# Attention scores added in PSUM to negated maxima that ScalarE copies there

## The reference, cut to what matters

```python
q = (x @ Wq).reshape(b, s, N_HEADS, HEAD_DIM)
k = (x @ Wk).reshape(b, s, N_HEADS, HEAD_DIM)
v = (x @ Wv).reshape(b, s, N_HEADS, HEAD_DIM)
dot = jnp.einsum('bihd,bkhd->bhik', q, k)
w = jax.nn.softmax(dot / jnp.sqrt(jnp.float32(HEAD_DIM)), axis=-1)
a = jnp.einsum('bhij,bjhd->bihd', w, v)
return a.reshape(b, s, N_HEADS * HEAD_DIM) @ Wo + bo
```

## Time and profile before

| | us |
|---|---|
| median of 3 runs | 1869.91 (1866.15 to 1872.6) |
| the profiled execution | 1864.58 |
| its span | 1863.3 |
| first add to the start of the last in the attention | 438.9 to 1703.1 |

### The profile page before, as it was taken

How to read it: one execution, slowest core, us unless ns; L and a number is a source line. 1 busy time by engine, 2 the same in 40 slices (tenths; PEclk the granted TensorE clock), 3 DMA queues, 4 the chain that set the end, 5 groups by cost and what they waited for, 6 DMA issues and landing times.

```text
span 1863.3 us, 34439 instructions
## 1 busy us (share of the span) xinstructions
PE 1660.9 (89%) x13785; PEld 979.6 (53%) x13785; DVE 1191.0 (64%) x1984; ACT 805.3 (43%) x1235; POOL 1306.9 (70%) x670
## 2 busy tenths in 40 slices
PE   4888852858999999999999999999999999995695
PEld 3666641745555555555555555555555555553475
DVE  2666666566666766666766666766666766653476
ACT  2555520444444444444444444444444444443223
POOL 2333322415988988988889888889888999995422
PEclk9877755879999999999999999999999999997698
DMA  8000000210000000000000000000000000000312
GB/s 244 4 3 3 4 1 16 64 33 1 1 1 1 1 1 1 1 1 1 1 1 1 1 1 1 1 1 1 1 1 2 1 1 1 1 1 28 98 41 73
DMA packets 33238, 29.76 MB, mean 16 GB/s; under 512 B 3676, under 2 KB 28752, under 8 KB 33080
## 3 DMA queue, kind: packets, MB, share of 16 engines
q1 hardware_dynamic: 24664, 19.38, 3.5%
q0 software_dynamic: 2496, 5.13, 0.8%
q10 hardware_dynamic: 5920, 3.04, 0.8%
HBM read 18.33 MB, written 9.21 MB: 15 GB/s over the span
## 4 chain that ended last, share of the span: by engine, by line
PE 79%; DVE 9%; POOL 6%; issue 3%; ACT 2%; DMA 1%; ACTq 1%; POOLq 0%; DVEq 0%; SPq 0%
PE psum L1895 24%; PE psum L1880 18%; PE psum L1853 9%; PE psum L1877 6%; POOL a_acc L2181 3%; PE psum L1525 2%; PE psum L1903 2%; PE psum L1826 2%; PE psum L1487 1%; POOL y_rows L1090 1%; DVE a_mx L2060 1%; PE psum L465 1%; PE psum L1535 1%; PE psum L375 1%; PE psum L470 1%
## 5 line engine op out<-in xcount | busy, mean ns | idle before, releaser
L2181 POOL TENSOR_TENSOR a_acc<-a_acc,a_Pb 128x1024 f32<-128x1024 f32 x448 | 1066.5, 2380 | 115.9 <-ACT a_Pb L1997 60.4
L2060 DVE TENSOR_REDUCE a_mx<-psum 128x2 f32<-128x1024 f32 x512 | 626.0, 1225 | 372.2 <-PE psum L1853 369.4
L1997 ACT ACTIVATE a_Pb<-psum 128x1024 f32<-128x1024 f32 x512 | 497.7, 1024 | 568.9 <-PE psum L1880 568.9
L1895 PE MATMUL psum<-a_Pb,a_Vb 128*64 128x512 f32 x2048 | 494.1, 603 | 0.0
L1895 PEld LDWEIGHTS psum<-a_Pb,a_Vb 128*64 128x64 f32 x2048 | 127.0, 136 | 231.4 <-issue 180.1
L1853 PE MATMUL psum<-a_Kh,a_Qh 64*128 64x512 f32 x1024 | 234.1, 451 | 5.4 <-DVE a_mx L2060 5.1
L1853 PEld LDWEIGHTS psum<-a_Kh,a_Qh 64*128 64x128 f32 x1024 | 97.6, 184 | 229.6 <-issue 219.9
L1877 PE MATMUL psum<-a_Mr,a_ones_r 64*128 64x512 f32 x1024 | 203.3, 392 | 0.0
L1880 PE MATMUL psum<-a_Ql,a_Kh 64*128 64x512 f32 x1024 | 202.4, 390 | 0.0
L1880 PE MATMUL psum<-a_Qh,a_Kh 64*128 64x512 f32 x1024 | 202.2, 390 | 0.0
L1880 PE MATMUL psum<-a_Qh,a_Kl 64*128 64x512 f32 x1024 | 201.8, 388 | 0.0
(11 more groups left out here) (393 smaller groups left out, 1944.2 us busy)
## 6 DMA issues: line engine op xcount, KB each, us to landing
x_rows<-att_raw ACTq DMA_DIRECT2D x2, 1483.5 KB, 24.4
g_w<-in_L_ffn_w_eDF_dram SPq DMA_DIRECT2D x2, 1408.0 KB, 9.0
r_W<-in_L_ffn_W_dram SPq DMA_DIRECT2D x1, 2048.0 KB, 14.0
r_tile_x<-x_rows SPq DMA_DIRECT2D x23, 64.5 KB
g_tile_x<-x_rows SPq DMA_DIRECT2D x23, 64.5 KB
y_all<-y_rows SPq DMA_DIRECT2D x4, 256.0 KB, 4.3
g_w<-in_L_ffn_w_eFD_dram SPq DMA_DIRECT2D x2, 512.0 KB, 10.2
g_xg<-y_rows SPq DMA_DIRECT2D x4, 256.0 KB, 3.7
```

What stands on the lines that cost most here:

```text
L1895: last = pe.matmul(ps[HEAD[h], B_O, :], b.Vb[:, p // 2 % 2, kc, at], b.Pb[:, step % BUFS, h * QT:(h + 1) * QT], start=(kc == 0), stop=(kc ...
L1997: act.activation(b.Pb[:, step % BUFS, :], ps[:, slot:slot + 2, :].rearrange("p a b -> p (a b)"), ACT.Exp, scale=SCALE).then_inc(S["probs"], 1)
L2060: v.tensor_reduce(b.mx[:, :, qc, quarter:quarter + 1], ps[:, bank:bank + 2, :], AX.X, ALU.max).then_inc(S[f"free{bank}"], 1)
L2181: g.tensor_tensor(b.acc[:, u, :], before, b.Pb[:, step % BUFS, :], ALU.add).then_inc(S["added"], 1)
```

## The change

The product of ones with `Mr` goes, and with it `Mr`, `ones`, `mask` and VectorE's multiplication. A score tile instead begins as a copy of the negated maxima that already lies in its banks, and the three products a head are added to it (no product of a step has `start=True`).

- At d = 7 TensorE writes the next unit's negated maxima into banks 0 and 1 with eight products of 128 columns (`seed`: a column of `nm`, broadcast, times the unit matrix). It waits for the exponential that reads these banks last. This seeds step 0 of the unit. For the first unit sixteen products fill both slots.
- ScalarE copies the two banks to SBUF (`guard`, into `Mb`, two buffers).
- For every other step ScalarE copies `Mb` into the banks of the step, behind the exponential that emptied them (`seed` of ScalarE): after the two exponentials of a round it seeds both slots for the next.
- VectorE's four reciprocals come a place earlier (d = 1, 2, 2, 3 instead of 2, 2, 3, 3); between the last of them and `normalise` there is now a reduction.
- VectorE could seed steps too, but the set `SEED_DVE` that names them is empty.

```diff
-            if R:
-                pe.wait_ge(S["probs"], 2 * R - 1 + i)
-            for h in range(2):
-                pe.matmul(ps[:, slot + h, :], b.ones[HEAD[h], :], b.Mr[HEAD[h], :], start=True, stop=False)
+            who, n = plan.seeded[2 * R + i]
+            if who != "pe":
+                pe.wait_ge(S[f"seeded_{who}"], n)
...
-                    last = pe.matmul(ps[:, slot + h, :], K[HEAD[h], p % 2, at], Q[HEAD[h], U % 3, :], start=False, stop=(n == 2))
+                    last = pe.matmul(ps[:, slot + h, :], K[HEAD[h], p % 2, at], Q[HEAD[h], U % 3, :], start=False, stop=(n == 2), skip_group_check=True)
...
-    def mask(U):
-        if U == 0:
-            pe.wait_ge(S["ident_r"], 1)
+    def seed(U):
+
         pe.wait_ge(S["negated"], U + 1)
-        bank = begin(("mask", U))
-        end(pe.matmul(ps[:, bank, 0:P], b.nm[:, :], b.ident[:, :], start=True, stop=True), bank)
+        begin(("seed", U))
+        if U:
+            pe.wait_ge(S["probs"], NT * U - 1)
+        else:
+            pe.wait_ge(S["free2"], plan.before[2])
+        for first in ((0, 2) if U == 0 else (0,)):
+            for h in range(2):
+                for qc in range(4):
+                    last = pe.matmul(ps[:, first + h, qc * P:(qc + 1) * P], bcast(b.nm[:, h, qc:qc + 1], [P, P]), b.ident[:, :],
+                                     start=(qc == 0), stop=(qc == 3), skip_group_check=True)
+        end(last, 0)
...
+    def guard(U):
+        bank = begin(("seed", U))
+        if U > 1:
+            for who in ("act",):
+                act.wait_ge(S[f"seeded_{who}"], max(n for step, (w, n) in plan.seeded.items() if w == who and step < NT * (U - 1)))
+        act.activation(b.Mb[:, U % 2, :], ps[:, 0:2, :].rearrange("p a b -> p (a b)"), ACT.Copy).then_inc(S[f"free{bank}"], 1)
+
+    def seed(step):
+        U, slot = step // NT, 2 * (step % 2)
+        if plan.seeded[step][0] == "act":
+            bank, n = plan.at["seed", U]
+            act.wait_ge(S[f"free{bank}"], n)
+            act.wait_ge(S["probs"], step - 1)
+            act.activation(ps[:, slot:slot + 2, :].rearrange("p a b -> p (a b)"), b.Mb[:, U % 2, :], ACT.Copy).then_inc(S["seeded_act"], 1)
...
+        if seed_job(R):
+            guard(U + 1)
+        for step in (2 * R + 2, 2 * R + 3):
+            if step < STEPS:
+                seed(step)
...
         if U and d in (2, 3):
-            invert(U - 1, 2 * d - 4)
+            invert(U - 1, 2 * d - 3)
         if U and d == 4:
             normalised_low(U - 1)
         if early:
             maximum(*early[1:])
-        if U and d in (2, 3):
-            invert(U - 1, 2 * d - 3)
+        if U and d in (1, 2):
+            invert(U - 1, 2 * d - 2)
+        if 2 * R + 3 < STEPS:
+            seed(2 * R + 3)
```

More of the change, by code:

```diff
@@ L1696, in misc_job, with seed_job @@
         return "v", p // 2 + 1, U % RN
-    if d == 7 and U < UNITS - 1:
-        return "mask", U + 1
-    return None
+    return None
+def seed_job(R):
+    U, d = R // RN, R % RN
+    return ("seed", U + 1) if d == 7 and U < UNITS - 1 else None
 def max_jobs(R):
@@ L1705, in max_jobs, with seeder @@
     return [("max", U, 2 * i + j) for j in range(2)] if U < UNITS else [None, None]
+SEED_DVE = ()
+def seeder(step):
+    if step % NT == 0 or step == 1:
+        return "pe"
+    return "dve" if step % 2 and (step // 2 - 1) % RN in SEED_DVE else "act"
 class Plan:
@@ L1723, in __init__ @@
                 self.job(("v", 0, m // 2), (B_O, B_P)[m // 2 % 2])
-        self.job(("mask", 0), B_P)
+        self.job(("seed", 0), 0)
         for key in max_jobs(-1):
@@ L1734, in __init__ @@
                 self.job(misc_job(R), B_P)
+            if seed_job(R):
+                self.job(seed_job(R), 0)
+        self.seeded, n = {}, {"pe": 0, "act": 0, "dve": 0}
+        for step in range(STEPS):
+            who = seeder(step)
+            n[who] += 1
+            self.seeded[step] = who, n[who]
         for key in (("sum", UNITS - 1), ("out", UNITS - 1)):
@@ L1766, in allocate_attention @@
     b.Qh, b.Ql = (sb(a, [P, 3, QT], F32R) for a in ("Qh", "Ql"))
-    b.Mr = sb("Mr", [P, QT], F32R)
-    b.ones = sb("ones_r", [P, P], F32R)
-    b.mask = sb("mask", [P, 4, P])
+    b.Mb = sb("Mb", [P, 2, 2 * QT])
     b.Vb = sb("Vb", [P, 2, NT, 2 * P])
@@ L1867, in scores @@
         if d == 0:
-            freed(("mask", U))
+            freed(("seed", U))
             freed(("q", U))
@@ L1915, in misc @@
         kind, *at = key
-        {"k": keys, "out": output, "sum": sums, "v": values, "q": queries, "mask": mask}[kind](*at)
+        {"k": keys, "out": output, "sum": sums, "v": values, "q": queries}[kind](*at)
     pe.wait_ge(S["tile_yt"], SLOTS_T)
@@ L1935, in attention_pe @@
             values(0, m // 2)
-    mask(0)
+    seed(0)
     for _, U, m in max_jobs(-1):
@@ L1950, in attention_pe @@
             misc(misc_job(R))
+        if seed_job(R):
+            seed(*seed_job(R)[1:])
         if R:
@@ L2017, in attention_act @@
         values(0, j)
+    guard(0)
     for R in range(ROUNDS):
@@ L2066, in negate, with seed @@
         if U:
-            bank, n = plan.at["mask", U - 1]
+            bank, n = plan.at["seed", U - 1]
             v.wait_ge(S[f"full{bank}"], n)
[L2069 to L2075, removed]
+        v.tensor_reduce(b.nm[:, :, :], b.mx[:, :, :, :], AX.X, ALU.max, negate=True).then_inc(S["negated"], 1)
+    def seed(step):
+        U, slot = step // NT, 2 * (step % 2)
+        if plan.seeded[step][0] == "dve":
+            bank, n = plan.at["seed", U]
+            v.wait_ge(S[f"free{bank}"], n)
+            v.wait_ge(S["probs"], step - 1)
+            v.tensor_copy(ps[:, slot:slot + 2, :].rearrange("p a b -> p (a b)"), b.Mb[:, U % 2, :]).then_inc(S["seeded_dve"], 1)
     def invert(U, part):
@@ L2140, in attention_dve @@
             maximum(*early[1:])
-        if U and d in (2, 3):
-            invert(U - 1, 2 * d - 3)
+        if U and d in (1, 2):
+            invert(U - 1, 2 * d - 2)
+        if 2 * R + 3 < STEPS:
+            seed(2 * R + 3)
         key = misc_job(R)
-        if key and key[0] in ("q", "k", "mask", "out"):
-            {"q": queries, "k": keys, "mask": mask, "out": output}[key[0]](*key[1:])
+        if key and key[0] in ("q", "k", "out"):
+            {"q": queries, "k": keys, "out": output}[key[0]](*key[1:])
         if U and d == 3:
```

12 lines of the change are left out of this document (3 added, 9 removed).

## The result

| | before | after |
|---|---|---|
| median of six runs, us | 1870.5 (1858.0 to 1874.0) | 1879.0 (1871.6 to 1880.6) |
| profiled execution, us | 1864.6 | 1877.9 |
| first add to end of the last, us | 1266.6 | 1275.0 |
| one unit, sums to sums (mean of 14), us | 40.00 | 40.29 |

The ratio of after to before is 1.0053, with a 95% interval of 1.0028 to 1.0078. The forecast was 1823 us. The table has two quantities that I use from here on. The stages ahead of the attention have nearly the same code in all kernels, yet the first add began anywhere from 438.9 to 451.2 us. So kernels are compared by the time from the first add to the end of the last, and by the unit in the middle of the run, as a mean of 14. Single units lie within 0.04 us of it before the change and within 0.03 after.

The account below looks back on a forecast made before the run. TensorE was taken as the bound, with GpSimd's adds close behind as a 37.9 us floor. 1864.6 - 55.2 (GpSimd's idle) + 0.2 x 32 + 2 at the start = 1818, plus 5.3 to the median: 1823 us, range 1807 to 1850.

Parts of the forecast that it names:

- TensorE's round: Bare rounds (d = 2 and 3): TensorE's products take 3.9 us, level with ScalarE's 3.9 from scores to scores.
- in the others TensorE has 0.9 us more to do, which covers it: Rounds with another job: TensorE's 0.9 us of extra products hide ScalarE's chain of exponentials and seed.
- Up to five copies of 512 columns: ScalarE's other copies in a unit: 2.5 us at a pitch of 0.50, within ScalarE's total of 32.5 us.
- the floor: GpSimd's fifteen adds a unit, each waiting for the one before: no unit under 37.9 us, whatever other engines do.
- the seed's price on ScalarE: One ScalarE copy of 1024 columns from SBUF into PSUM: taken as 0.96 us, about 1.0 to 1.05 alone.
- the seeding products: TensorE's eight products of 128 columns a unit: 0.9 us taken, 0.5 to 1.1 possible; sixteen at the start, 3.2 us.
- the wait at d = 7 of about 0.35: At d = 7 TensorE's seeding products wait about 0.35 us for the round's first exponential, and no more is lost.
- VectorE's line from the sums to the subtraction: Reciprocals, reductions, normalising and ScalarE's copy: the subtraction that frees bank 7 comes 13.4 us after the sums.
- rival 4: TensorE's clock falls to 1.2 GHz in places; a tenth of its time there gives 41.8 us a unit, 1926; chance 0.04.
- the query product waits for the subtraction, 0.5 to 1.0 a unit: Sign of a right forecast: TensorE's query product waits 0.5 to 1.0 us a unit for VectorE to free bank 7.
- The slower side: Chance 0.10 of a slower run: drawn-out ScalarE writes to PSUM, a falling TensorE clock, or a share of eaten savings.
- Rival 1: Hand-overs between ScalarE and TensorE make bare rounds 4.2 to 4.4 us and a unit 39.0; 1848 us, chance 0.17.

Follow-up runs that it names:

- the half reductions: The changed kernel with each maximum reduced over the first 256 of 512 columns of either bank: one run, 1830.0 us, a unit of 38.63 us.

## Why the prediction was wrong

**The step that failed is the one on TensorE's round**: "TensorE's shortest round is 0.43 + 1.38 + 0.23 + 1.87 = 3.9" and "in the others TensorE has 0.9 us more to do, which covers it". The round was added up from TensorE's products and compared with ScalarE's chain. The loop through VectorE was never closed for an ordinary round. The rows had most of it. The late product starts at 1002.61 and its reduction ends at 1004.31, 1.70 us later, against the 0.43 + 1.38 = 1.81 that TensorE works before the early product. That leaves 0.11 for a hand-over, which no row there shows and the prediction put at nothing. Measured after the change by the starts of the products: 1.77 us to the end of the reduction and 0.14 of hand-over make 1.91, against 1.74 of work, a wait of 0.17, and the weighing behind it comes another 0.11 late. The 0.9 us of the other job cover none of it, for they stand behind the early product.

The prediction had followed this line only from the sums to the query product. That piece came out as forecast, 13.57 us against 13.5, and the waits at d = 2 and 3 lie inside it. At d = 7 the wait for the exponential covers the loop, and this round took 5.28 with the half reductions too. What the loop adds to a unit is about 0.3 us in each of the four rounds at d = 5, 6, 0 and 1: some 1.2 us, and 1.36 with all that shorter reductions gave (39.30 to 37.94).

**A second step is missing altogether.** The seeds were priced by what they make late on TensorE (the scores), not by what they stand ahead of on ScalarE. "Up to five copies of 512 columns" entered the sum as work; that keys and queries pass from them to VectorE, with a reduction queued behind, was not asked. Measured: 0.99 us a unit, the whole of the second pattern.

With both the unit is 40.29 - 0.99 - 1.36 = 37.94, the floor. GpSimd's floor left 2.06 us a unit to win (40.00 to 37.94). TensorE's own work fell far enough to win them, but the two waits put 2.35 on top of the floor, 0.29 more than there was to win.

What held: the floor itself (37.9 forecast; 37.94 measured, but only in a run that leaves half of each maximum out); the seed's price on ScalarE (1.03 alone, 0.95 as the second of two); the seeding products (1.01 against 0.9, and 3.16 us for the sixteen at the start against 3.2); the wait at d = 7 of about 0.35; VectorE's line from the sums to the subtraction (13.51 against 13.4); the clock, 1.00 throughout with TensorE 97% busy, so rival 4 was rightly small. The Trainium skill (TensorE: Matmul & The Clock Gate, A second HAM failure mode: psum-queue depth-cycling) reports a clock that swung with short idles between groups of products; here it stayed at 1.00 with waits of 0.2 to 0.6 us behind the reductions. What did not hold is the sign "the query product waits for the subtraction, 0.5 to 1.0 a unit": it starts 0.06 behind the subtraction's end, but comes so late for the waits before it that only 0.07 of wait is left.

**The rivals.** The slower side, 0.10, was given to slow writes to PSUM and to the clock; neither happened. Rival 1 had bare rounds of 4.2 to 4.4, near the measured 4.15 and 4.21, but for another reason, which makes that luck; its 0.9 us a unit is under half of the 2.2 that the unit came out above 38.1. What it was excused with, 0.9 us of slack in six rounds of eight, is the same wrong step. The case that came, an engine other than the two compared closing a loop, had no rival. The range was built from the prices of added work, which were nearly all right, and held none for an interval that the removed work had covered.

## What to carry to other kernels

Before crediting the removal of work on the bounding engine, list what ran beside it: for each buffer that this engine fills twice a round, add product, reader and hand-over, and compare it with what is left between the two fills. An engine with 35% idle time can close such a loop. And when work is put into an engine's stream, ask of each instruction behind it who waits for it and what is queued behind that waiter: moving three copies won 0.99 us a unit, where the whole change had cost 0.29.

## What the runs showed of the hardware

- A ScalarE copy from SBUF into PSUM of 128x1024 fp32 took 1.03 us, and 1.98 for two in a row, beside a TensorE busy 97% of the time.
- Products added to banks that ScalarE had filled, none of them with `start=True`, gave the reference's result, after TensorE had written the same banks before. With seeds in only 128 of 512 columns the result was another, so what lies in the banks is added to.
- A change from pairs of 64-row products to products of 128 rows, or back, cost about 0.1 us around the output products: 0.32 from start to start instead of 0.23; a lone pair in between held its place for 0.43.
- TensorE started 0.14 us after the end of the reduction it waited for, and the weighing behind it came 0.43 after that start instead of 0.32. With the reduction split in two the product started 0.06 us after the end of the second part, and the query product started 0.06 us after the subtraction.
